# A graph network's edge-list search: bf16 one-hots from doubled keys, and five long gathers in place of fifty

## The chip, the core and the metric

The kernel runs on one core of a Trainium2 chip. The metric is the device time of one execution, in microseconds (us); the time of a kernel is the median over its runs. The engines are TensorE (PE; its weight loads are listed as PEld), VectorE (DVE), ScalarE (ACT), GpSimd (POOL) and the queue engine SyncE (SP), which only issues transfers here.

## The reference, cut to what matters

Four graph layers run one after the other on 3,125 nodes with 128 features; each is a layer norm and a ReLU, a layer, and a residual sum. The graph has 103,125 edges, given as `src` and `dst`, sorted by `dst`:

```python
edge_index = jnp.stack([src, dst])
h = jnp.maximum(_layernorm(x, axis=-1), 0.0)
x = x + _L0_gnn_ref(h, edge_index, L0_gnn_W, L0_gnn_b)          # degree-normalized sum over edges
h = jnp.maximum(_layernorm(x, axis=-1), 0.0)
x = x + _L1_gnn_ref(h, src, dst, L1_gnn_Wq, L1_gnn_Wk, L1_gnn_Wv)  # 4 attention heads over edges
h = jnp.maximum(_layernorm(x, axis=-1), 0.0)
x = x + _L2_gnn_ref(h, edge_index, edge_weight, ...)            # two weighted layers
h = jnp.maximum(_layernorm(x, axis=-1), 0.0)
x = x + _L3_gnn_ref(h, edge_index, edge_attr_16, ...)           # messages from edge attributes
```

All of them need to know which edges end in which node. The change touches only how the kernel finds and fetches these lists at its start.

## The kernel before, in words

The program is a row of blocks. Between two blocks all engines meet at a barrier. Inside a block every engine has its own stream of instructions, ordered by hand with semaphores.

**Block 1, `window_starts` (L157 to L327), finds where each window's edges begin.** A window is five neighbouring destination nodes, and there are 625 windows. The sorted `dst` is loaded as 125 partitions x 825 columns. SP issues that load and the load of `x`, then the copies of `src`, `dst` and `edge_weight` into `scratch_table` in memory (4,125 rows of 3 x 25 values, L315), then one border edge for each partition (L318) and two edges of each edge group (L320, L321), which add to `ends_in`, and last the table's padding (L322). DVE casts `dst` to f32, works out the window of each edge with two `floor_div`s (L113, L114), and splits it into `win_hi` (0 to 24) and `win_lo` (0 to 24, L239). In five pieces of 165 columns it compares both with 0 to 24 (L244), which makes the bf16 one-hots `one_hi` and `one_lo`. Each DVE operation is "linked": the engine waits for its semaphore before the next. For each piece PE multiplies the one-hots, five columns at a time (`GRP`), into `pairs_ps` (L294, 33 matmuls a piece). Then DVE waits for `ends_in`, makes three small tests of the input (`falls`, `wide`, L253 to L257), waits for PE, masks `pairs` (L260), and a short chain of small operations of DVE and PE gives the first table row of each window (L265 to L274), which SP writes to `scratch_starts` (L325).

**Block 2, `edge_slots` (L370 to L505), fetches each window's edges.** SP loads the starts (L419) and then the layers' weights. POOL makes three iotas and waits for `index`. DVE waits for the iotas and the starts and works out `index` = start + 0 to 9 (L445). Then POOL issues 50 gathers (L433), for each of `BLOCKS` = 5 blocks of 125 windows ten (`GROWS`), each of which fetches one table row of 75 values (300 bytes) for each of 125 partitions:

```python
            for b in range(BLOCKS):
                for j in range(GROWS):
                    nc.gpsimd.indirect_dma_start(rows[:, b, j, :], None, table, ...)
```

Meanwhile DVE runs the first layer norm (`layer_norm_relu`, L130 to L139) and keeps the transposed weights (`keep_weights`, L362 to L367); ACT scales the normalized rows (L153). Then, for each block b, DVE waits for its gathers and copies them out to `flat` (L456, three copies), PE transposes `flat` in two halves of three transposes (L486) into two halves of PSUM, and ACT copies each half out (L498, three copies). PE waits before half n until ACT has copied half n - 2. When all are copied, DVE makes the keys and weights (L459 to L474).

**Block 3, `adjacency` (L508 on),** builds the count matrices in bf16. It starts with the first comparison into `hot` (L607), which reads bf16 keys stored twice next to each other and bf16 `steps`. After it come the layers; nothing in them is touched.

## Time and profile before

| | |
|---|---|
| Time, median of 3 runs | 3521.36 us (3520.54 to 3534.1) |
| The profiled execution's own time | 3524.91 us |
| Its span, first to last instruction | 3523.2 us |
| Busy: PE, DVE, ACT, POOL | 2461.0, 1738.8, 1209.0, 1837.8 us |
| First comparison of the `adjacency` block starts at | 166.75 us |

The profiled execution's time is 1.71 us longer than its span and 3.55 us (0.1%) above the median. All places in time are microseconds from the start of the span. Busy shares over the whole span tell little here: the stages of the program follow one another, and each has its own limit.

### The profile page before, as it was taken

To read this page: it belongs to the slowest core of one execution; us is meant where nothing else is said; L and a number is where in the kernel's file an instruction comes from. 1 tells how busy PE (TensorE), PEld (TensorE's weight loads), DVE (VectorE), ACT (ScalarE), POOL (GpSimd) and SP (SyncE) were. 2 spreads that over 40 slices of the span, in tenths; PEclk is the share of its full clock that TensorE was granted. 3 is DMA by queue.
4 is the path that set the end of the run, shared out by engine and by line. 5 is a ranking of instruction groups with operands and counts; after the bars stand their busy time and mean duration, and the time that the engine had idled before them with its cause. 6 is when DMAs were issued, how large, how long until landed. Compare 5 with 4: busy or idle time off the path is not lost. (4 is left out here: it accounts for less than half of the span.)

```text
span 3523.2 us, 60853 instructions
## 1 busy us (share of the span) xinstructions
PE 2461.0 (70%) x19676; PEld 1710.3 (49%) x19676; DVE 1738.8 (49%) x3577; ACT 1209.0 (34%) x2123; POOL 1837.8 (52%) x1601
## 2 busy tenths in 40 slices
PE   2176776768588878878779998266666666666666
PEld 2166666634255555555554454144444444444444
DVE  8399999934487787888871113111111111111112
ACT  1166666611587787787860001000000000000000
POOL 2500000000688888888840000377777777777776
PEclk7599999979699999999999998555555555555555
DMA  4045555573211111111119784312222222222122
GB/s 50 17 146 180 177 177 177 176 202 98 71 49 43 46 46 47 44 49 45 46 43 231 182 203 94 46 48 48 48 48 49 48 48 48 48 49 48 48 48 57
DMA packets 243639, 296.72 MB, mean 84 GB/s; under 512 B 151910, under 2 KB 185517, under 8 KB 240267
## 3 DMA queue, kind: packets, MB, share of 16 engines
q1 hardware_dynamic: 175120, 239.72, 26.6%
q0 software_dynamic: 68400, 55.69, 6.6%
q8 instruction: 41, 0.67, 0.1%
q14 instruction: 78, 0.64, 0.1%
HBM read 191.87 MB, written 103.70 MB: 84 GB/s over the span
## 5 line engine op out<-in xcount | busy, mean ns | idle before, releaser
L2047 POOL DMA_INDIRECT gathered_rows<-scratch_projected,index x825 | 997.6, 1209 | 310.3 <-issue 213.7
L1617 POOL TENSOR_TENSOR score<-score,rise 125x500 f32<-125x500 f32 (+1 forms) x609 | 672.2, 1139 | 44.8 <-DVE peaks L1553 40.8
L2104 PE MATMUL sums<-hot,message 125*128 125x32 f32 x1650 | 386.2, 403 | 360.7 <-DVE message L2131 360.7
L2104 PEld LDWEIGHTS sums<-hot,message 125*128 125x128 f32 x1650 | 364.2, 329 | 514.3 <-DVE message L2131 346.3
L1617 POOL TENSOR_TENSOR H<-H,rise 125x500 f32<-125x500 f32 (+1 forms) x91 | 103.3, 1135 | 818.2 <-DVE peaks L1553 815.6
L2095 PE MATMUL factor<-mix,attrT 80*125 80x320 f32 x660 | 412.0, 778 | 57.7 <-ACT attrT L2065 57.7
L2065 ACT COPY attrT<-attr_flipped 80x125 f32<-80x125 f32 x165 | 43.0, 260 | 1181.2 <-PE attr_flipped L2091 1181.2
L2131 DVE TENSOR_TENSOR message<-gathered_rows,factor 125x640 f32<-125x640 f32 x165 | 135.5, 821 | 592.3 <-DMA gathered_rows<-scratch_projected,index 592.3
L1553 DVE CUSTOM_DVE_ANT_0 score<-raw,log_in 125x500 f32<-125x500 f32 (+1 forms) x609 | 353.9, 619 | 133.4 <-PE raw L1438 80.7
L1453 PE MATMUL probsT<-ident,score 125*125 125x125 f32 x2175 | 349.5, 288 | 30.5 <-ACT score L1509 12.4
L1500 ACT ACTIVATE rise<-raw 125x1000 f32<-125x1000 f32 (+1 forms) x350 | 313.9, 917 | 150.3 <-DVE peaks L1553 77.6
L1453 PEld LDWEIGHTS probsT<-ident,score 125*125 125x125 f32 x2175 | 289.2, 195 | 107.8 <-DVE weighed L1574 66.6
L667 PE MATMUL built<-pair_weight,hot 125*128 125x125 bf16 x3750 | 256.7, 232 | 113.9 <-DVE pair_weight L614 113.9
L667 PEld LDWEIGHTS built<-pair_weight,hot 125*128 125x128 bf16 x3750 | 234.7, 105 | 131.8 <-DVE pair_weight L614 131.8
L614 DVE TENSOR_TENSOR pair_weight<-hot,w_parts 125x3840 bf16<-125x3840 bf16 x125 | 269.7, 2158 | 17.2
L2095 PEld LDWEIGHTS factor<-mix,attrT 80*125 80x125 f32 x660 | 191.0, 320 | 172.1 <-ACT attrT L2065 105.7
L1438 PE MATMUL raw<-QT,key 32*125 32x500 f32 (+1 forms) x1400 | 194.4, 625 | 92.1 <-DVE peaks L1553 89.1
L1574 DVE COPY weighed<-probsT 125x500 f32<-125x500 f32 x400 | 251.0, 672 | 13.9 <-PE probsT L1453 13.9
L1509 ACT ACTIVATE score<-score,shift 125x3125 f32<-125x3125 f32 x87 | 252.5, 2903 | 0.0
L2137 DVE TENSOR_TENSOR acc<-acc,sums 128x32 f32 x165 | 31.1, 188 | 421.4 <-PE sums L2104 421.4
L1964 POOL MEMSET mix<- 80x640 f32 x1 | 0.6, 628 | 392.9 <-POOLq L1168 392.9
L607 DVE TENSOR_TENSOR hot<-keys,steps 125x2560 bf16<-125x2560 bf16 x125 | 185.5, 1484 | 0.3 <-PEq L375 0.3
(225 smaller groups left out, 3266.2 us busy)
## 6 DMA issues: line engine op xcount, KB each, us to landing
weights_in<-scratch_weightsT SPq DMA_DIRECT2D x50, 1093.8 KB
scratch_weightsT<-wT SPq DMA_DIRECT2D x25, 1367.2 KB
scratch_logs<-log SPq DMA_DIRECT2D x75, 437.5 KB
log_in<-scratch_logs SPq DMA_DIRECT2D x150, 218.8 KB
counts_in<-scratch_counts SPq DMA_DIRECT2D x25, 683.6 KB
scratch_counts<-cc SPq DMA_DIRECT2D x24, 683.6 KB
gathered_rows<-scratch_projected,index POOLq DMA_INDIRECT x825, 3.3
attr<-in_edge_attr SPq DMA_DIRECT2D x165, 39.1 KB
```

The lines of the kernel that those rows point to most:

```text
L614: nc.vector.tensor_tensor(pair_weight[:, b].rearrange("p k g (a e) -> p k g a e", e=2), pair.unsqueeze(1).broadcast_to([P, 3, G, FULL // 2 ...
L667: ins = nc.tensor.matmul(built[b][:, 256 * w + P:256 * w + 2 * P], hot[:, q, 0, 2 * w + h], pair_weight[:, b, k, 2 * w + h, 0:P], start=(h ...
L1438: ins = nc.tensor.matmul(raw[:, h, 0:w], key[head, u, :], QT[head, at:at + w], start=True, stop=True)
L1453: ins = nc.tensor.transpose(probsT[:, b, h * P:(h + 1) * P], score[u][h][:, a * P:(a + 1) * P], ident[0:P, 0:P])
L1500: nc.scalar.activation(rise[:, b, heads, 0:width[g]], raw[:, heads, 0:width[g]], ACT.Relu, scale=1.0 / SLOPE - 1.0).then_inc(risen, 1)
L1509: nc.scalar.activation(score[u][h], score[u][h], ACT.Exp, bias=shift[:, u, h:h + 1], accum_out=total[:, u, h:h + 1]).then_inc(exped, 1)
L1553: nc.vector.tensor_tensor_reduce(out=score[u][h][:, at:at + w], in0=raw[:, h, 0:w], in1=log_in[:, at:at + w], scale=1.0, scalar=-3e38, op0 ...
L1574: nc.vector.tensor_copy(weighed[:, a % RING].rearrange("p h d -> p (h d)"), probsT[:, a % 3, 0:PW]).then_inc(moved_dve, 1)
L1617: nc.gpsimd.tensor_tensor(score[u][h][:, at:at + w], score[u][h][:, at:at + w], rise[:, b, h, 0:w], ALU.add).then_inc(added, 1)
L2047: nc.gpsimd.indirect_dma_start(gathered[:, u, k, :], None, projected, bass.IndirectOffsetOnAxis(ap=index[:, u, k:k + 1], axis=0)).then_inc ...
L2095: ins = nc.tensor.matmul(factor[u][:, h, 0:EG * D // 2], attrT[:, u, :], mix[:].rearrange("r c d -> r (c d)")[:, h * EG * D // 2:(h + 1) * ...
L2104: ins = nc.tensor.matmul(sums[:], message[:, u, k, :], hot[:, u, k, :], start=(k == 0), stop=(k == EG - 1))
```

## The change

In block 1 the keys `win_hi` and `win_lo` are written as bf16, each value twice next to itself (`key_hi`, `key_lo`). The comparisons read these and a bf16 iota, in pairs of elements; they make rows of 26 columns instead of 25. The columns are padded from 825 to 828 with keys of -1, and cut into nine pieces of 92. The comparisons are no longer linked to one another: each adds to `ones_made`. PE takes four columns a matmul (104 x 104) instead of five (125 x 125), so 23 matmuls a piece and 207 in all instead of 165. In block 2 each window's ten table rows, which lie next to one another in memory, are fetched as one run of 750 values (3,000 bytes) from a view of the table as single elements, so there are five gathers. `index` is the start times 75, and the iota, the two casts and the sum that made the ten indices are gone.

```diff
+    JOINT, PIECES = 4, 9
+    WIDE = TILES + 1
+    PADDED = (CHUNKS + JOINT - 1) // JOINT * JOINT
+    SIDE = JOINT * WIDE
...
-        one_hi = e(nc.sbuf_tensor(unique("one_hi"), [P, CHUNKS, TILES], BF16))
-        one_lo = e(nc.sbuf_tensor(unique("one_lo"), [P, CHUNKS, WPT], BF16))
+        key_hi = e(nc.sbuf_tensor(unique("key_hi"), [P, PADDED, 2], BF16))
+        key_lo = e(nc.sbuf_tensor(unique("key_lo"), [P, PADDED, 2], BF16))
+        one_hi = e(nc.sbuf_tensor(unique("one_hi"), [P, PADDED, WIDE], BF16))
+        one_lo = e(nc.sbuf_tensor(unique("one_lo"), [P, PADDED, WIDE], BF16))
+        iota_short = e(nc.sbuf_tensor(unique("iota_short"), [P, WIDE], BF16))
...
             dve.wait_ge(pool_done, 11)
+            nc.vector.tensor_copy(iota_short[:], iota_i[:, 0:WIDE])
+            nc.vector.memset(key_hi[:, CHUNKS:, :], -1.0)
+            nc.vector.memset(key_lo[:, CHUNKS:, :], -1.0)
...
             floor_div(nc, link, win_hi[:], win_lo[:], WPT)
-            link(nc.vector.scalar_tensor_tensor(win_lo[:], win_hi[:], -float(WPT), win_lo[:], ALU.mult, ALU.add))
-            step = CHUNKS // 5
-            for k in range(5):
+            both = lambda x: x[:].unsqueeze(2).broadcast_to([P, CHUNKS, 2])
+            link(nc.vector.tensor_copy(key_hi[:, 0:CHUNKS, :], both(win_hi)))
+            link(nc.vector.scalar_tensor_tensor(key_lo[:, 0:CHUNKS, :], both(win_hi), -float(WPT), both(win_lo), ALU.mult,
+                                                ALU.add))
+            step = PADDED // PIECES
+            each = iota_short[:].rearrange("p (a e) -> p a e", e=2).unsqueeze(1).broadcast_to([P, step, WIDE // 2, 2])
+            for k in range(PIECES):
                 part = slice(k * step, (k + 1) * step)
-                for one, win in ((one_hi, win_hi), (one_lo, win_lo)):
-                    link(nc.vector.tensor_tensor(one[:, part, :],
-                                                 win[:, part].unsqueeze(2).broadcast_to([P, step, TILES]),
-                                                 iota[:, 0:TILES].unsqueeze(1).broadcast_to([P, step, TILES]),
-                                                 ALU.is_equal))
-                marks["one", k] = count[0]
+                for one, key in ((one_hi, key_hi), (one_lo, key_lo)):
+                    nc.vector.tensor_tensor(one[:, part, :].rearrange("p c (a e) -> p c a e", e=2),
+                                            key[:, part].unsqueeze(2).broadcast_to([P, step, WIDE // 2, 2]), each,
+                                            ALU.is_equal).then_inc(ones_made, 1)
...
-            per = CHUNKS // GRP
+            per = PADDED // JOINT
             for k in range(per):
-                if k % (per // 5) == 0:
-                    pe.wait_ge(dve_done, marks["one", k // (per // 5)])
+                if k % (per // PIECES) == 0:
+                    pe.wait_ge(ones_made, 2 * (k // (per // PIECES) + 1))
...
-            nc.gpsimd.iota(off_i[:], [[1, GROWS]], base=0, channel_multiplier=0).then_inc(pool_ready, 1)
...
+            runs = table.rearrange("r (e o) -> (r e) o", o=1)
             pool.wait_ge(index_ready, 1)
             for b in range(BLOCKS):
-                for j in range(GROWS):
-                    nc.gpsimd.indirect_dma_start(rows[:, b, j, :], None, table,
-                                                 bass.IndirectOffsetOnAxis(ap=index[:, j, b:b + 1], axis=0)
-                                                 ).then_inc(gathered[b], 16)
+                nc.gpsimd.indirect_dma_start(rows[:, b].rearrange("p j r -> p (j r)"), None, runs,
+                                             bass.IndirectOffsetOnAxis(ap=index[:, b:b + 1], axis=0)
+                                             ).then_inc(gathered[b], 16)
...
-            dve.wait_ge(pool_ready, 3)
+            dve.wait_ge(pool_ready, 2)
             nc.vector.tensor_copy(steps[:], steps_i[:])
-            link(nc.vector.tensor_copy(off_f[:], off_i[:]))
             dve.wait_ge(loaded, 16)
-            link(nc.vector.tensor_copy(row_f[:], row0[:]))
-            nc.vector.tensor_tensor(index[:], row_f[:].unsqueeze(1).broadcast_to([P, GROWS, BLOCKS]),
-                                    off_f[:].unsqueeze(2).broadcast_to([P, GROWS, BLOCKS]),
-                                    ALU.add).then_inc(index_ready, 1)
+            nc.vector.tensor_scalar(index[:], row0[:], float(KINDS * ROW), None, ALU.mult).then_inc(index_ready, 1)
...
             for b in range(BLOCKS):
-                dve.wait_ge(gathered[b], 16 * GROWS)
+                dve.wait_ge(gathered[b], 16)
```

The masks `fold` and `same`, `pairs` and the two PSUM tiles behind it change from 125 to 104 columns, and `hist` (L265) sums four blocks of 26 columns instead of five of 25.

## Rows read from the trace of the kernel before

**Rows 1.** Stretches: us, busy and count of PE, PEld, DVE, ACT, POOL; clock, DMA share, GB/s.

```profile
8.90:53.80 44.90, 15.11 (x132) 14.37 (x132) 44.58 (x10) 0.00 (x0) 0.00 (x0) 0.78 0.63 37
84.80:148.40 63.60, 8.11 (x30) 6.67 (x30) 3.51 (x16) 6.05 (x31) 47.15 (x39) 0.50 0.13 24
166.75:3523.20 3356.45, 2431.41 (x19465) 1683.99 (x19465) 1647.53 (x3420) 1189.31 (x2063) 1771.51 (x1533) 0.76 0.34 87
```

**Rows 2.** Timeline of block 1: start us, us, engine, line, operation, tiles, count.

```profile
4.72 0.59 DVE L236 CAST win_lo<-dst_i 125x825 f32<-125x825 int32 x1
...
7.85 1.02 DVE L239 SCALAR_TENSOR_TENSOR win_lo<-win_hi,win_lo 125x825 f32<-125x825 f32 x1
...
8.90 4.46 DVE L244 TENSOR_TENSOR one_hi<-win_hi,iota 125x4125 bf16<-125x4125 f32 x1
...
24.96 7.99 SPq L318 DMA_DIRECT2D dst_i<-in_dst  x1
...
34.53 0.81 SPq L321 DMA_DIRECT2D ends_i<-in_dst  x1
35.38 0.51 SPq L322 DMA_DIRECT2D scratch_table<-pad  x1
...
49.33 4.46 DVE L244 TENSOR_TENSOR one_lo<-win_lo,iota 125x4125 bf16<-125x4125 f32 x1
53.83 1.02 DVE L253 TENSOR_TENSOR falls<-dst_i 125x825 f32<-125x825 int32 x1
...
53.84 3.79 PE L294 MATMUL pairs_ps<-one_lo,one_hi 125*125 125x125 bf16 x33 [5.21 <-DVE one_lo L244]
...
56.32 0.15 DVE L257 TENSOR_REDUCE faults<-wide 33x1 f32<-33x5 f32 x1
57.74 0.29 DVE L260 TENSOR_TENSOR pairs<-pairs_ps,same 125x125 f32<-125x125 f32 x1 [1.27 <-PE pairs_ps L294]
```

**Rows 3.** Two more stretches of block 1, columns as in rows 1.

```profile
37.20:37.40 0.20, 0.20 (x5) 0.20 (x4) 0.20 (x1) 0.00 (x0) 0.00 (x0) 0.50 0.71 6
37.40:37.60 0.20, 0.20 (x5) 0.20 (x4) 0.20 (x1) 0.00 (x0) 0.00 (x0) 0.50 0.02 0
```

**Rows 4.** The comparisons of block 3: ns min/median/max, first and last start us.

```profile
L607 DVE TENSOR_TENSOR hot<-keys,steps x125: 1480/1484/1493, 166.8 to 707.5; 125x2560 bf16<-125x2560 bf16 x125
```

**Rows 5.** Timeline of block 2, columns as in rows 2.

```profile
67.33 0.21 DVE L445 TENSOR_TENSOR index<-row_f,off_f 125x50 int32<-125x50 f32 x1
67.46 2.41 DVE L130 BATCH_NORM_STATS2 stats<-X 125x6 f32<-125x128 f32 x12
...
67.87 1.41 POOL L433 DMA_INDIRECT rows<-scratch_table,index  x1 [1.12 <-DVE index L445]
...
80.42 3.90 ACT L153 ACTIVATE H<-H,rstd 125x128 f32<-125x128 f32 x13 [2.78 <-DVE rstd L139]
...
81.87 0.41 DVE L367 TENSOR_TENSOR bias<-parts 1x256 f32<-1x256 f32 x1
...
84.83 0.49 DVE L456 CAST flat<-rows 125x250 f32<-125x250 int32 x2 [2.55 <-DMA rows<-scratch_table,index]
...
85.57 1.62 PE L486 MATMUL turned<-ident,flat 125*125 125x125 f32 x6 [16.36 <-DVE flat L456]
...
87.55 0.29 ACT L498 COPY weight<-turned 125x125 f32<-125x125 f32 x1
```

**Rows 6.** The gathers: ns min/median/max, first and last start us; time to landing.

```profile
L433 POOL DMA_INDIRECT rows<-scratch_table,index x50: 1205/1209/1405, 67.9 to 142.3; - x50
...
DMA to landing us min/median/max: 2.8/3.0/3.2
```

**Rows 7.** DMA engines in 40 slices of 85.5 to 87.1 us: busy share, tenths.

```profile
DMA  0062000000000000000000000000292289000002
```

**Rows 8.** Timeline where the last block of windows has been copied.

```profile
148.38 0.81 DVE L459 CAST outside<-win_i 125x1250 f32<-125x1250 int32 x1 [2.35 <-ACT weight L498]
```

More of the change, by code:

```diff
@@ L157, in window_starts @@
 def window_starts(nc, T, table, starts, X, ident, ones, iota, iota_tile, irregular):
+    JOINT, PIECES = 4, 9
+    WIDE = TILES + 1
+    PADDED = (CHUNKS + JOINT - 1) // JOINT * JOINT
+    SIDE = JOINT * WIDE
+    assert PADDED % (JOINT * PIECES) == 0 and WPT == TILES
     used = []
@@ L177, in window_starts @@
         iota_ti = e(nc.sbuf_tensor(unique("iota_ti"), [P, TILES], I32))
-        fold = e(nc.sbuf_tensor(unique("fold"), [P, TILES], F32))
-        same = e(nc.sbuf_tensor(unique("same"), [P, GRP], F32))
+        fold = e(nc.sbuf_tensor(unique("fold"), [SIDE, WIDE], F32))
+        same = e(nc.sbuf_tensor(unique("same"), [SIDE, JOINT], F32))
         before = e(nc.sbuf_tensor(unique("before"), [TILES, TILES], F32))
-        pairs = e(nc.sbuf_tensor(unique("pairs"), [P, P], F32))
+        pairs = e(nc.sbuf_tensor(unique("pairs"), [SIDE, SIDE], F32))
         hist = e(nc.sbuf_tensor(unique("hist"), [TILES, WPT], F32))
@@ L196, in window_starts @@
         pe_done = sem("pe_done")
+        ones_made = sem("ones_made")
         starts_done = sem("starts_done")
@@ L288, in _ @@
         def _(pe):
-            per = CHUNKS // GRP
+            per = PADDED // JOINT
             for k in range(per):
-                if k % (per // 5) == 0:
-                    pe.wait_ge(dve_done, marks["one", k // (per // 5)])
-                ins = nc.tensor.matmul(pairs_ps[:], one_hi[:, GRP * k:GRP * (k + 1), :].rearrange("p j h -> p (j h)"),
-                                       one_lo[:, GRP * k:GRP * (k + 1), :].rearrange("p j h -> p (j h)"),
-                                       start=(k == 0), stop=(k == per - 1))
+                if k % (per // PIECES) == 0:
+                    pe.wait_ge(ones_made, 2 * (k // (per // PIECES) + 1))
+                here = slice(JOINT * k, JOINT * (k + 1))
+                ins = nc.tensor.matmul(pairs_ps[:], one_hi[:, here, :].rearrange("p j h -> p (j h)"),
+                                       one_lo[:, here, :].rearrange("p j h -> p (j h)"), start=(k == 0),
+                                       stop=(k == per - 1))
             ins.then_inc(pe_done, 1)
@@ L378, in edge_slots @@
         row0 = e(nc.sbuf_tensor(unique("row0"), [P, BLOCKS], I32))
[L379 to L382 removed]
+        index = e(nc.sbuf_tensor(unique("index"), [P, BLOCKS], I32))
         rows = e(nc.sbuf_tensor(unique("rows"), [P, BLOCKS, GROWS, KINDS * ROW], I32))
```

18 lines of the change are left out of this document (7 added, 11 removed).

## The prediction

> **What bounds the kernel now.** I read the timeline first, since the blocks are separated by barriers and busy shares over 3,500 us say nothing of a start that is 5% long. Everything from the first comparison of block 3 at 166.75 us to the end is untouched [rows 1], so the question is how much earlier that instruction starts. I then took each block's start apart by stretches, and asked in each which engine the others wait for.
>
> Block 1 is DVE's: in the 44.90 us from 8.90 to 53.80 us DVE is busy 44.58 with ten comparisons, PE 15.11 [rows 1]. One comparison takes 4.46 us, the ten run end to end, and only then come the three tests (53.83 to 56.47 us); PE's last piece starts at 53.84, takes 3.79 us, and `pairs` (L260) starts at 57.74 after waiting 1.27 us for it [rows 2]. Block 2 is POOL's: from 84.80 to 148.40 us POOL is busy 47.15 of 63.60 us, no other engine over 8.2 [rows 1], and the 50 gathers start from 67.9 to 142.3 us, so one each (142.3 - 67.9)/49 = 1.52 us, of which 1.21 is the instruction [rows 6]. The reader should see in the timeline that layer norm and weights end on DVE at 81.87 + 0.41 = 82.28 us, 2.55 us before the first block of windows is there [rows 5]; after that everybody waits for gathers up to 148.38 us [rows 8].
>
> **Block 1: the comparisons.** Prices first. On f32 keys DVE takes 1.02 us for 825 elements and 4.46 for 4,125 [rows 2]: (4.46 - 1.02)/3,300 = 1.042 ns an element and 0.16 us fixed. The comparison of block 3, which has just the form that the change brings (bf16 in doubled pairs), takes 1.484 us for 2,560 elements [rows 4], less 0.16 that is 0.517 ns each. A new comparison has 92 x 26 = 2,392 elements: 1.40 us. If the pairs bought nothing it would be 2.65. I take 1.40, since form, types and the innermost pair are those of rows 4. Without links the next instruction starts 0.08 us before the last ends: `index` starts at 67.33, takes 0.21, and the next starts at 67.46 [rows 5]. So 18 comparisons take 17 x 1.32 + 1.40 = 23.8 us, against 44.9.
>
> What comes before them: three small unlinked instructions (iota copy, two memsets), at 0.1 us each by the smallest row, 0.15 [rows 2], less the overlap: +0.3, at most 0.45. The keys' cast has 1,650 elements; the cast of 825 takes 0.59 [rows 2], (0.59 - 0.16)/825 = 0.52 ns, so 1.02 us and at most 1.88 at the slow price. I take 1.02, the same kind of operation. `key_lo` is a two-source f32 operation like L239, 1,650 elements: 1.88 in place of 1.02. From 4.72: +0.3, then 3.13 unchanged up to 8.15, 1.06 and 1.92 with their links: the first comparison starts at 11.1 (8.90 before), the last ends at 34.9, at the latest 35.9.
>
> PE: 33 matmuls take 3.79 us, 0.115 each [rows 2]; 23 take 2.6 at that price, 2.2 if they shrink with the columns (104 of 125). DVE makes a piece in 2 x 1.32 = 2.64, so PE keeps up at either price, though at 2.6 only just, and ends by 34.9 + 2.6 = 37.5.
>
> **The wait that comes next.** After its last comparison DVE waits for `ends_in`. Before, this had long come. Now it hasn't: SP issues the last of these transfers only at 34.53 to 35.34 us, because its queue stands behind the table copies (L318 alone holds it 7.99 us) [rows 2], and the DMA engines are still 0.71 busy at 37.3 us and quiet from 37.4 [rows 3]. None of this depends on DVE. Behind this wait on DVE lie the tests and with them `pairs`, and PE waits for that. The landing lies between 35.4 and 37.6; I take 37.3, since these few small packets are queued behind the table's on the same engines. Then the tests, 2.64 us, and `pairs` at 40.0 us, against 57.74: **-17.7 us**. This also covers every uncertainty of DVE's list up to 2.4 us. If the landing were early PE's 37.5 and DVE's 34.9 + 2.64 would be last: `pairs` at 37.6, -20.1. The chain behind `pairs` stays; 104 columns for 125 save less than 0.1.
>
> **Block 2: up to the first gather.** One small iota (POOL) and two small casts (DVE, linked) go, 0.15 + 0.04 us each by the smallest row [rows 2]: some -0.5 us, at most 0.6, nothing if the load of the starts is the last to come. So in the old clock the first gather starts at 67.3, layer norm at 66.9 and DVE is free at 81.7.
>
> **The gathers.** Neither their number of rows per instruction (125) nor POOL's work for one changes if each partition's run is one piece, so 1.52 us apart the five start at 67.3 to 73.4. Each moves 375,000 bytes. Bounds for the transfer: now 42 gathers in 63.60 us at a DMA share of 0.13 [rows 1] cost 0.13 x 16 x 63.6/42 = 3.15 engine-us each for 37,500 bytes; ten times that is 31.5, or 2.0 us on 16 engines. After 166.75 us the engines move 87 GB/s at a share of 0.34, 16 GB/s each [rows 1], so 23.4 engine-us, 1.5 us. With 3.0 us from start to landing as now [rows 6], the last is there at 73.4 + 3.0 + 1.5 = 77.9, or at 67.3 + 3.0 + 5 x 2.0 = 80.3. I take the middle, 79; either is before DVE is free at 81.7. So layer norm, which was hidden behind gathers, becomes the cover, and the transfers cost nothing. If they were twice as slow, the last would come at 90 and still just in time for the fifth block.
>
> Do all 16 engines share a gather? In one slice of 0.04 us the busy share reaches 9 tenths [rows 7], 14 engines at once. The Trainium skill, "DMA: Bandwidth & Descriptors", in "Why a DMA increments its semaphore by 16 and not by 1", says that a DMA uses the largest number up to 16 that divides its outer dimension, here 5 of 125. The trace does not agree for the gathers as they are; by the rule a long gather would take 31.5/5 = 6.3 us at the dearer price.
>
> **From the gathers to the keys.** DVE copies block after block without waiting: three copies in 0.69 us (84.83 on) [rows 5], the first is done at 82.4. PE needs 1.62 for two halves, and ACT ends 87.84 - 85.57 = 2.27 us after PE's start: 1.62 and 0.65 behind it [rows 5]. ACT is free of layer norm only at 84.32 - 0.6 = 83.7, so half 0 is copied at 84.35. Half n waits for the copy of half n - 2, which costs 0.81 (PE) + some 0.25 + 0.6 (ACT) = 1.7 for two halves: four more rounds, 84.35 + 6.8 = 91.15, and half 9 at 92.0. L459, before at 148.38 [rows 8], starts at 92.1: **-56.3 us**. Bounds: PE alone as limit gives 91.2; every block one after the other, 83.7 + 5 x 2.3 = 95.2.
>
> **Sum.** -17.7 - 56.3 = -74.0 us. The first comparison of block 3 starts at 92.7 instead of 166.75. The profiled execution ran 3524.91, so a like one 3450.9; the median is 3.55 lower: **3447.3 us**, -2.1%. Differences under 0.5% (17.6 us) could hardly be told from no change here; this one can.
>
> **The rivals.**
>
> *The wait for `ends_in` costs nothing* (landing before 35 us): 20.1 for 17.7, 3445 us. For it: the transfers are tiny. Against it: issue ends at 35.34, and the engines are full till 37.4 [rows 2, 3]. Chance 0.08.
>
> *Late gathers.* Each pays ten times today's engine time and only five engines carry all: 5 x 31.5/5 = 31.5 us, last landing at 67.3 + 3 + 31.5 = 102, then one block's 3 us: L459 at 105, 3460 us. Against it rows 7. Every engine count between gives less. Chance 0.12 for 3452 to 3475.
>
> *The doubled keys don't do what they should*: comparisons of 2.65 us, 17 x 2.57 + 2.65 = 46.3, end at 57.4, tests, `pairs` at 60.1: block 1 loses 2.4 us, and the total is -53.9: 3467 us. For it: the inner run is 26 columns where that of rows 4 is 128. Chance 0.06.
>
> *The other side: a long gather is cut into single elements.* The new view of the table has a last dimension of 1. If each value becomes a transfer of its own, there are 468,750. In block 1 the 100-byte rows of the table, under 12,400, took 0.63 x 16 x 44.9 = 453 engine-us [rows 1], 37 ns each; 468,750 x 37 ns/16 = 1,080 us, so some 4,450 us in all, more if POOL pays 1.21/125 us for each. It decides against the change as soon as the five gathers take over 96 us (last landing at 163 instead of 145 in the old clock, which eats block 1's gain). Against it: the destination is one run of 3,000 bytes a partition, and in rows 6 75 values travel at one price per row. The Trainium skill, "DMA: Bandwidth & Descriptors", in the same section, says that one descriptor moves one contiguous run of the last dimension; read on the source alone, that speaks for this rival, and no row here tests it. Chance 0.04.
>
> **How the numbers follow.** The forecast as told has 0.70, its own range 3444 to 3452 (PE's lower bound and noise below, 95.2 for 92.1 above). With the early landing (0.08) and the nearer two thirds of the late gathers (0.08), 3440 to 3462 holds about 0.86 on paper; what I leave out are the slow comparisons, the elements and the far end of the late gathers. All but the elements are faster by over 0.5%: 0.95; slower 0.04; within 0.5% 0.01, for long gathers at 60 to 90 us in all.
>
> **What would show it.** Right: 18 comparisons of 1.40 us, the last ending near 35 us; DVE idle for `ends_in` for some 2 us; `pairs` at 40; five gathers of 1.2 us on POOL, no wait of DVE for them after 81.7 in the old clock; L459 some 8 us after the end of ACT's second scaling; block 3 from 92.7 us on as before. Wrong: comparisons of 2.6 us, PE as the releaser of `pairs`, a wait of `flat` on gathers, or a gather on POOL well over 1.5 us. The prediction also fails if later stages don't move along rigidly, for instance at another granted clock; nothing in the rows ties them to a place in time.

## The result, and the profile after

The time fell from 3526.73 us (3520.54 to 3534.1, four runs in all) to 3473.39 us (3469.66 to 3475.32), a ratio of 0.9858 [0.984, 0.9875]: 53 us less, where 74 had been forecast. The direction was right; the size was not, and 3473 lies above the range given. The brackets behind a ratio are its 95% interval.

Block 1 after: the timeline of the changed kernel, with start, duration, and in brackets the idle time and its releaser.

```profile
7.87 1.87 DVE L252 CAST key_hi<-win_hi 125x1650 bf16<-125x1650 f32 x1
9.78 1.88 DVE L253 SCALAR_TENSOR_TENSOR key_lo<-win_hi,win_lo 125x1650 bf16<-125x1650 f32 x1
11.69 1.41 DVE L260 TENSOR_TENSOR one_hi<-key_hi,iota_short 125x2392 bf16<-125x2392 bf16 x1
...
26.20 10.52 SPq L333 DMA_DIRECT2D dst_i<-in_dst  x1
...
34.04 1.40 DVE L260 TENSOR_TENSOR one_lo<-key_lo,iota_short 125x2392 bf16<-125x2392 bf16 x1
...
35.49 1.31 PE L309 MATMUL pairs_ps<-one_lo,one_hi 125*104 125x104 bf16 x23 [0.88 <-DVE one_lo L260]
36.77 1.22 SPq L335 DMA_DIRECT2D ends_i<-in_dst  x1
38.03 0.81 SPq L336 DMA_DIRECT2D ends_i<-in_dst  x1
38.88 0.51 SPq L337 DMA_DIRECT2D scratch_table<-pad  x1
43.27 1.02 DVE L267 TENSOR_TENSOR falls<-dst_i 125x825 f32<-125x825 int32 x1 [7.83 <-DMA ends_i<-in_dst]
...
45.94 0.27 DVE L274 TENSOR_TENSOR pairs<-pairs_ps,same 104x104 f32<-104x104 f32 x1
```

The comparisons take 1.40 us and the last ends at 35.44. PE takes 1.31 us for its last piece, and `pairs` doesn't wait for it. DVE then stands 7.83 us for `ends_in`. The issue of the border edges starts 1.2 us later than before and holds SP for 10.52 us where it took 7.99 [rows 2], so the last of these transfers is issued at 38.84 us instead of 35.34. `pairs` starts at 45.94 instead of 57.74: 11.8 us earlier, 17.7 forecast.

Block 2, same view.

```profile
55.19 0.16 DVE L453 TENSOR_SCALAR index<-row 125x5 int32<-125x5 int32 x1
...
55.68 1.41 POOL L443 DMA_INDIRECT rows<-scratch_table,index  x1 [0.67 <-DVE index L453]
...
61.98 1.21 POOL L443 DMA_INDIRECT rows<-scratch_table,index  x1 [0.30 <-issue]
...
69.37 0.41 DVE L382 TENSOR_TENSOR bias<-parts 1x256 f32<-1x256 f32 x1
69.71 0.47 DVE L462 CAST flat<-rows 125x250 f32<-125x250 int32 x2
...
79.95 0.81 DVE L465 CAST outside<-win_i 125x1250 f32<-125x1250 int32 x1 [7.18 <-ACT weight L504]
...
98.33 1.49 DVE L613 TENSOR_TENSOR hot<-keys,steps 125x2560 bf16<-125x2560 bf16 x1 [0.30 <-PEq L390]
```

The five gathers go as forecast, and the first copy into `flat` follows layer norm with no wait. The keys start 79.95 - 45.94 = 34.0 us after `pairs`, before 148.38 - 57.74 = 90.6 [rows 2, 8]: -56.6 us, forecast -56.3. The gathers' own rows:

```profile
L443 POOL DMA_INDIRECT rows<-scratch_table,index x5: 1209/1213/1407, 55.7 to 62.0; - x5
...
DMA to landing us min/median/max: 7.2/7.5/7.8
```

So the last landed near 61.98 + 7.5 = 69.5 us (an estimate from the median), about when DVE was free. What the transfers used, from the DMA queues between 55 and 71 us (packets, MB, share of 16 engines):

```profile
q0 software_dynamic: 1120, 1.88, 38.4%
```

0.384 x 16 x 16 / 5 = 19.7 engine-us a gather.

Block 3 starts at 98.33 instead of 166.75 us, 68.4 earlier, yet the span fell only by 49.6. The missing 19 us are lost later. From the start of block 3 to the first gather of the edge layer at the end (L2053) it was 2090.1 us and is now 2109.8, and most of that lies in the attention layer, from whose first to last score product it was 890.1 and is 904.8 us. The change doesn't touch this layer. Stretches of 800 us inside it show every engine executing fewer instructions after the change; first before, then after (columns as in rows 1).

```profile
952.00:1752.00 800.00, 645.69 (x7845) 449.20 (x7845) 641.33 (x1770) 633.17 (x709) 685.43 (x623) 0.96 0.17 46
```

```profile
884.00:1684.00 800.00, 646.29 (x7746) 451.10 (x7746) 627.18 (x1742) 621.61 (x700) 673.58 (x613) 0.94 0.17 45
```

No engine is full in either: the busiest, POOL, has 685.43 of 800 us before. TensorE's granted clock, the third value from the end, is lower as well, 0.94 for 0.96. DVE's waits in the same stretches (us in total, times, longest), before and after:

```profile
DVE score L1553 <- issue: 25.2, 14, 2.8
```

```profile
DVE score L1559 <- issue: 30.6, 30, 2.9
```

"Issue" means that nothing which the profile shows holds the engine. Below stand one such row of after (with the one ahead of it), and what the instruction queue q14 moved (packets, MB, share) in those stretches, first before and then after. No view names the engine that q14 serves. I take the packets that differ between kernels for DVE's, since edits of DVE's stream alone change their number (e16 and e17 below).

```profile
1347.04 0.68 DVE L1580 COPY weighed<-probsT 125x500 f32<-125x500 f32 x1
1350.37 0.68 DVE L1559 CUSTOM_DVE_ANT_0 score<-raw,log_in 125x500 f32<-125x500 f32 x1 [2.65 <-issue]
```

```profile
q14 instruction: 56, 0.46, 0.2%
```

```profile
q14 instruction: 55, 0.45, 0.2%
```

This made three theories; the lower clock could be a cause of its own or follow from any of them. **Position**: later stages run slower when they start at another time. **TensorE's stream**: block 1 has 42 more matmuls, so its code lies elsewhere. **VectorE's stream**: the change lengthens DVE's program ahead of block 3 by 8 instructions (45 to 56 in block 1, 121 to 118 in block 2, counted in the program, its waits included), and the attention loop, 330 DVE instructions for two tiles, lies 8 places further on.

### The profile page after: what moved, and what is told of

Same layout as the page of the kernel before. It is cut to its first block and busy times, and to the rows that moved or that the text cites. A ratio compares the mean times of both kernels' runs of the same rounds, so it can differ in the third digit from the quotient of the medians.

```text
span 3473.6 us, 60900 instructions
## 1 busy us (share of the span) xinstructions
PE 2475.7 (71%) x19718; PEld 1722.4 (50%) x19718; DVE 1719.1 (49%) x3587; ACT 1208.9 (35%) x2123; POOL 1782.4 (51%) x1555
## 5 line engine op out<-in xcount | busy, mean ns | idle before, releaser
L2053 POOL DMA_INDIRECT gathered_rows<-scratch_projected,index x825 | 997.0, 1208 | 310.3 <-issue 213.9
L1444 PE MATMUL raw<-QT,key 32*125 32x500 f32 (+1 forms) x1400 | 196.8, 632 | 93.9 <-DVE peaks L1559 90.6
L1580 DVE COPY weighed<-probsT 125x500 f32<-125x500 f32 x400 | 251.0, 672 | 13.4 <-PE probsT L1459 13.1
L2143 DVE TENSOR_TENSOR acc<-acc,sums 128x32 f32 x165 | 31.2, 189 | 421.6 <-PE sums L2110 421.6
```

Source lines behind the costliest of these rows:

```text
L1444: ins = nc.tensor.matmul(raw[:, h, 0:w], key[head, u, :], QT[head, at:at + w], start=True, stop=True)
L1580: nc.vector.tensor_copy(weighed[:, a % RING].rearrange("p h d -> p (h d)"), probsT[:, a % 3, 0:PW]).then_inc(moved_dve, 1)
L2053: nc.gpsimd.indirect_dma_start(gathered[:, u, k, :], None, projected, bass.IndirectOffsetOnAxis(ap=index[:, u, k:k + 1], axis=0)).then_inc ...
```

## The experiments

Each kernel was timed beside the kernel before. "DVE" is the number of DVE instructions added ahead of block 3. "Start saved" is 167.0 us (the mean of 166.75 and 167.2 in two profiles of before) less the start of block 3; "time saved" is the median of before in the same batch less the kernel's (3526.73 for after; 3524.61 for e1 to e4, 3523.95 for e5 to e8, 3528.52 for e9 to e12, 3525.58 for e13 to e16, 3525.32 for e17 and e18); "given back" is the difference of the two. "Attention" is first to last score product in the profile. The start is that of one profiled execution and the times are medians, so a difference of a few us between two entries of "given back" says nothing; the profiled executions of e7 and e1 were 15 and 18 us slower than their medians.

| kernel | DVE | median us | ratio | block 3 starts | start saved | time saved | given back | attention |
|---|---|---|---|---|---|---|---|---|
| after | +8 | 3473.39 | 0.9858 [0.984, 0.9875] | 98.3 | 68.7 | 53.3 | 15.4 | 904.8 |
| e1_keys_alone | +11 | 3512.97 | 0.9967 [0.9953, 0.9981] | 153.6 | 13.4 | 11.6 | 1.8 | 908.8 |
| e2_gathers_alone | -3 | 3469.73 | 0.9845 [0.9828, 0.9862] | 110.1 | 56.9 | 54.9 | 2.0 | 886.5 |
| e3_after_again | +8 | 3465.94 | 0.9829 [0.9813, 0.9844] | 95.1 | 71.9 | 58.7 | 13.2 | 896.4 |
| e4_before_again | 0 | 3523.16 | 0.9999 [0.9987, 1.001] | 167.2 | -0.2 | 1.4 | -1.6 | 892.8 |
| e5_wait16 | +8 | 3483.66 | 0.9893 [0.9867, 0.9919] | 112.6 | 54.4 | 40.3 | 14.1 | 896.6 |
| e6_wait70 | +8 | 3540.26 | 1.0045 [1.0031, 1.006] | 169.0 | -2.0 | -16.3 | 14.3 | 899.1 |
| e7_ends_first | +8 | 3461.74 | 0.9822 [0.9805, 0.9838] | 90.8 | 76.2 | 62.2 | 14.0 | 901.7 |
| e8_not_doubled | +8 | 3484.91 | 0.9881 [0.9859, 0.9903] | 112.8 | 54.2 | 39.0 | 15.2 | 903.9 |
| e9_pe42 | -3 | 3473.76 | 0.9843 [0.9817, 0.9869] | 109.9 | 57.1 | 54.8 | 2.3 | 885.7 |
| e10_dve11 | +8 | 3482.79 | 0.986 [0.9834, 0.9886] | 110.2 | 56.8 | 45.7 | 11.1 | 896.1 |
| e11_pe86 | +8 | 3466.13 | 0.981 [0.9784, 0.9836] | 90.2 | 76.8 | 62.4 | 14.4 | 902.0 |
| e12_pe22 | +8 | 3463.7 | 0.9804 [0.9778, 0.9829] | 90.4 | 76.6 | 64.8 | 11.8 | 903.5 |
| e13_dve120 | +128 | 3456.61 | 0.9796 [0.9772, 0.982] | 90.2 | 76.8 | 69.0 | 7.8 | 887.8 |
| e14_three_pieces | -4 | 3453.79 | 0.9783 [0.9757, 0.9809] | 92.1 | 74.9 | 71.8 | 3.1 | 887.9 |
| e15_pool3 | +5 | 3448.99 | 0.9773 [0.9748, 0.9798] | 90.9 | 76.1 | 76.6 | -0.5 | 885.4 |
| e16_dve60 | +68 | 3416.74 | 0.9688 [0.9664, 0.9713] | 90.4 | 76.6 | 108.8 | -32.2 | 855.7 |
| e17_before68 | +68 | 3493.97 | 0.9914 [0.9894, 0.9934] | 166.8 | 0.2 | 31.4 | -31.2 | 853.0 |
| e18_after60 | +68 | 3431.03 | 0.9733 [0.9712, 0.9754] | 95.7 | 71.3 | 94.3 | -23.0 | 863.3 |

**The parts, and both kernels once more.** e1 is the changed `window_starts` with the old `edge_slots`, e2 the reverse; no line is edited otherwise.

> Only block 1 of the change (bf16 doubled keys, nine pieces, 104 columns); the fifty gathers as before. Shift of the first comparison of block 3, rigid: pairs at 46 as in the changed kernel instead of 57.7, so 11.8 us earlier. Interference theory (the faster comparisons slow the DMA engines beside them): the last border edges arrive at about 43 us again. Scatter theory (DMA time differs between executions): anywhere from 38 to 43. Clock theory by position: attention stage longer than 890 us; by scatter: 885 to 910, no relation. Time: 8 to 14 us below the kernel before.

> Only block 2 of the change (five long gathers); block 1 as before. Block 3 starts 56.7 us earlier. Interference theory: DMA engines quiet at 37.4 us as in the kernel before; scatter theory: 37 to 43. If nothing is given back later the time is 57 us below the kernel before; if the loss of the changed kernel after block 3 (19 us in its profile) comes from standing earlier in time, 40 to 45 us below.

> The changed kernel unaltered, for the scatter of its parts. Interference theory: border edges at 43 us again, block 3 from 98.3 us. Position theory of the clock: attention from the first to the last score product again 905 us and 314 us at the lower clock level between blocks 3 and the edge layer; scatter theory: both move by 10 us or more from execution to execution. Rigid shift alone would make it 68 us faster than the kernel before; its four runs so far say 50 to 54.

> The kernel before, unaltered, for the scatter of its parts. Position theory: attention again 890 us, 270 us at the lower level. Scatter theory: attention 885 to 910 us, the profile so far having been one of the short ones, since two of four runs were 12 us longer than the other two. Time equal to the kernel before within its scatter of 14 us.

The gathers alone move the end as far as the start of block 3, less 2.0 us; both parts together give back 13.2. The loss is no accident of one profile: the repeat of before keeps its time, the repeat of after gives back again. The keys alone don't fit so well: by the medians they give back 1.8 us only, yet in the profile the attention took 908.8. That profile is of the slowest of ten executions (3531.4; the others from 3506.01), so I rest nothing on its times. What it shows of DVE's waits stands in the last part of this section.

**Position, the wait for `ends_in`, and the doubled pairs.** e5 and e6 keep the changed code and hold POOL back in block 2, with 5 and 22 extra iotas:

```diff
+            wait = chained(pool, held)
+            for _ in range(5):
+                wait(nc.gpsimd.iota(win_i[:].rearrange("p (w h) -> p w h", h=2), [[WIN, WINDOWS], [0, 2]], base=0,
+                               channel_multiplier=0))
```

e7 issues `ends_in` before the table copies:

```diff
             start_rows(sp, X[:], T["x"].rearrange("(t p) f -> p t f", p=P), x_in)
-            for k, name in enumerate(("src", "dst", "edge_weight")):
-                column = table[0:ROWS, k * ROW:(k + 1) * ROW]
-                if name == "edge_weight":
-                    column = column.bitcast(F32)
-                sp.dma_start(column, T[name].rearrange("(r e) -> r e", e=ROW)).then_inc(table_done, 16)
             sp.wait_ge(pool_done, 11)
             with nc.allow_non_contiguous_dma(reason="an edge a row, and two of every edge group"):
...
                 sp.dma_start(ends_i[:, 1, :], grouped[:, :, EG * P - 1]).then_inc(ends_in, 16)
+            for k, name in enumerate(("src", "dst", "edge_weight")):
+                column = table[0:ROWS, k * ROW:(k + 1) * ROW]
+                if name == "edge_weight":
+                    column = column.bitcast(F32)
+                sp.dma_start(column, T[name].rearrange("(r e) -> r e", e=ROW)).then_inc(table_done, 16)
```

e8 compares with a key that isn't read in pairs:

```diff
-                    nc.vector.tensor_tensor(one[:, part, :].rearrange("p c (a e) -> p c a e", e=2),
-                                            key[:, part].unsqueeze(2).broadcast_to([P, step, WIDE // 2, 2]), each,
+                    nc.vector.tensor_tensor(one[:, part, :],
+                                            key[:, part, 0:1].broadcast_to([P, step, WIDE]),
+                                            iota_short[:].unsqueeze(1).broadcast_to([P, step, WIDE]),
```

> The changed kernel with five more linked iotas on GpSimd (3.3 us each) ahead of the index: block 3 starts some 16.5 us later, where it starts with the gathers alone (110 us). Position theory (what is lost after block 3 depends on where block 3 stands in time): no loss at this place, so 55 us below the kernel before, 5 us slower than the changed kernel. Added-work theory (the loss comes with the comparisons' change, whatever the place): 60 - 16 = 44 us below. Scatter alone: 44 to 50 below.

> The changed kernel with 22 more linked iotas: block 3 starts some 73 us later, at 168 us, where it starts in the kernel before (167). Position theory: the time of the kernel before within 2 us. Theory that the loss comes with the comparisons' change: 10 to 14 us slower than the kernel before. Scatter alone: equal within 3.

> The changed kernel with the three transfers for ends_in issued ahead of the table copies. The wait of VectorE for them (7.8 us in the profile) goes: tests start with the last comparison at 35.4 to 35.6, pairs at 38.2, so 2 to 7.7 us earlier, unless the table copies, now later, hold SP back before it writes the starts at 41. Time: 3 to 7 us below the changed kernel, 63 to 67 below the kernel before. If the wait had been covered anyway: no difference.

> The changed kernel, but the comparisons read each bf16 key once, repeated by a step of 0 over 26 columns, instead of doubled pairs. If the doubled pair is what makes the fast form: 2,392 x 1.042 ns + 0.16 = 2.65 us a comparison, the last ends at 11.7 + 46.3 = 58.0, pairs at 60.7, 15 us later than in the changed kernel and 3 us later than in the kernel before; time 12 to 18 us above the changed kernel. If bf16 alone is enough: 1.40 us a comparison and no difference.

Position falls. e6 starts block 3 two microseconds after the kernel before does, and still loses 16.3 us; wherever the code of after starts block 3, it gives back 13 to 15. Timeline of e7 and of e8, DVE:

```profile
34.29 1.40 DVE L260 TENSOR_TENSOR one_lo<-key_lo,iota_short 125x2392 bf16<-125x2392 bf16 x1
35.61 1.01 DVE L267 TENSOR_TENSOR falls<-dst_i 125x825 f32<-125x825 int32 x1
...
38.27 0.27 DVE L274 TENSOR_TENSOR pairs<-pairs_ps,same 104x104 f32<-104x104 f32 x1
```

```profile
55.23 2.64 DVE L260 TENSOR_TENSOR one_lo<-key_lo,iota_short 125x2392 bf16<-125x2392 bf16 x1
57.79 1.01 DVE L268 TENSOR_TENSOR falls<-dst_i 125x825 f32<-125x825 int32 x1
...
60.46 0.27 DVE L275 TENSOR_TENSOR pairs<-pairs_ps,same 104x104 f32<-104x104 f32 x1
```

With `ends_in` issued early the wait is gone and `pairs` starts at 38.27, 7.7 us before that of after. In time e7 beats e3 by 4.2 us, which the intervals don't separate. Without pairs a comparison takes 2.64 us and `pairs` starts at 60.46: the rival's 2.65 and 60.1. Then nobody waits for `ends_in`.

**Which stream.** e9 adds 42 small transposes on PE to e2, e11 and e12 86 and 22 of them to e7; e10 adds 11 memsets on DVE to e2.

```diff
+            for _ in range(42):
+                nc.tensor.transpose(spare[0:32, 0:32], ident[0:32, 0:32], ident[0:32, 0:32])
...
+            for k in range(11):
+                nc.vector.memset(spare[:, k:k + 1], 0.0)
             dve.wait_ge(pool_ready, 2)
```

> The kernel with the gathers alone (from the start of block 3 to the edge layer 2092 us), and 42 small transposes more on TensorE in block 2, where it is idle and nobody waits for it; their output is not read. It gives TensorE as many more instructions ahead of block 3 as the change gives it in block 1. Theory of the place in TensorE's instruction stream: the stretch from block 3 to the edge layer becomes 2102 to 2118 us and the time 10 to 16 us longer than with the gathers alone. Theory that VectorE's stream, the memory or the comparisons themselves do it: 2092 again and no difference.

> The kernel with the gathers alone and eleven small memsets more on VectorE at the start of block 2, where it waits 4.6 us for GpSimd; their output is not read. VectorE then has as many instructions ahead of block 3 as in the changed kernel. Theory of VectorE's instruction stream: from block 3 to the edge layer 2102 to 2118 us and 10 to 16 us longer than with the gathers alone. Theory of TensorE's stream: 2092, no difference.

> The changed kernel with the transfers for ends_in first, and 86 small transposes on TensorE in block 2 (output not read), so that with the 42 of block 1 TensorE has 128 matrix instructions more than the kernel before, each with its weight load. Theory of TensorE's stream, if it repeats with 256 instructions: from block 3 to the edge layer 2090 to 2093 us again and the time 12 to 16 us below the version without them, 3446 to 3450. Otherwise 2102 to 2118 and no gain, or 1 us lost if the transposes get in the way.

> The same with 22 small transposes: 64 matrix instructions more than the kernel before. Theory of TensorE's stream, if it repeats with 128 instructions: 2090 to 2093 us from block 3 to the edge layer, as with 86. If it repeats with 256 alone: 2102 to 2118. Other theories: no difference from the version without them.

TensorE's stream falls: 42 more PE instructions change nothing (2.3 given back, as in e2's 2.0), and 86 or 22 on top of +8 cure nothing (14.4 and 11.8). Eleven empty DVE instructions, executed long before, bring the loss into the kernel that hadn't it: 9.0 us more than e9, with the attention 10.4 us longer. The intervals of e9 and e10 overlap; what carries the reading is that all nine kernels with +8 give back 11 to 15 us, and the five with -4 to +5 from -1.6 to 3.1. By its times e1, at +11, doesn't join the first group (1.8).

**Other counts.** All on top of e7. e13 adds two lots of 60 memsets and e16 one. e14 cuts the comparisons into three pieces (`JOINT, PIECES = 4, 3`), twelve instructions fewer. e15 gives the three small preparations to GpSimd:

```diff
+            link(nc.gpsimd.tensor_copy(iota_short[:], iota_i[:, 0:WIDE]))
+            link(nc.gpsimd.memset(key_hi[:, CHUNKS:, :], -1.0))
+            link(nc.gpsimd.memset(key_lo[:, CHUNKS:, :], -1.0))
...
-            dve.wait_ge(pool_done, 11)
-            nc.vector.tensor_copy(iota_short[:], iota_i[:, 0:WIDE])
-            nc.vector.memset(key_hi[:, CHUNKS:, :], -1.0)
-            nc.vector.memset(key_lo[:, CHUNKS:, :], -1.0)
+            dve.wait_ge(pool_done, 14)
```

> The version with the transfers for ends_in first, and 120 small memsets on VectorE in block 2, 60 where it waits for GpSimd and 60 where it waits for ScalarE (output not read): 128 instructions more than in the kernel before. Theory that the place in VectorE's stream counts and repeats with 128: from block 3 to the edge layer 2090 to 2093 us instead of 2102 to 2118. Theory that any added instruction on VectorE costs it: 2102 to 2118. Time: 10 to 16 us below the version without them less what the memsets themselves cost (0 to 3 us), 3449 to 3455; else no gain.

> The version with the transfers first, and the comparisons in three pieces of 276 columns instead of nine of 92: twelve comparisons fewer, so VectorE has 4 instructions fewer than in the kernel before. Theory of the place in VectorE's stream: from block 3 to the edge layer 2090 to 2093 us. Price: TensorE's last piece has 69 matmuls (4 to 6.7 us) and ends after the tests, pairs 1 to 4 us later. Time 8 to 14 us below the version with nine pieces, 3450 to 3456. If the loss belongs to doubled keys or the earlier start: 1 to 4 us slower.

> The version with the transfers first, and its three small preparations (bf16 iota, two memsets) on GpSimd instead of VectorE: 5 instructions more on VectorE than in the kernel before. Theory of the stream: 2090 to 2093 or 2102 to 2118 from block 3 to the edge layer, according to where the border between -3, 0 (no loss) and +8, +11 (loss) lies; nothing between the two levels. In block 1 up to 0.5 us either way.

> The version with the transfers first, and 60 small memsets on VectorE where it waits for GpSimd (output not read): 68 instructions more than in the kernel before. Theory that it repeats with 64 instructions: about as with +4, unknown side; with 128: half a period off, most likely a loss, 2102 to 2118. Any-added-work theory: 2102 to 2118 or more.

e14 and e15 get back nearly all of the rigid gain (3.1 and -0.5 given back). e15 is e7 with three instructions moved from DVE to GpSimd, and the intervals of the two don't overlap: it is the clearest pair for the loss at +8. e13, at +128, has the attention of count 0 (887.8), but its time gives back 7.8, and from the start of block 3 to the edge layer it takes 2100.6 us where its expectation asked for 2090 to 2093: the attention repeats with 128, for the whole time that isn't shown. And e16, with 60 instructions that do nothing, is 45 us faster than e7: 3416.74 us, the fastest kernel here. Its expectation had called a loss most likely. Its attention stretch, DVE's wait for issue, and q14:

```profile
880.00:1680.00 800.00, 654.31 (x8234) 455.05 (x8226) 668.76 (x1851) 659.79 (x743) 716.25 (x651) 0.99 0.17 46
```

```profile
DVE score L1562 <- issue: 0.5, 1, 0.5
```

```profile
q14 instruction: 7, 0.06, 0.0%
```

In the same 800 us DVE executes 1,851 instructions for 1,742, it hardly ever waits for issue, and q14 moves 7 packets instead of 55. The memsets themselves cost nothing, since DVE waits for POOL right behind them (timeline of e16):

```profile
43.56 1.67 DVE L452 MEMSET spare<- 125x1 f32 x58 [0.38 <-issue]
47.13 0.23 DVE L454 CAST steps<-steps_i 125x128 bf16<-125x128 int32 x1 [1.89 <-POOL steps_i L440]
```

**The place alone, and the change at equal place.** The same memsets in the kernel before (68) and in after (60), with nothing else edited: both loops then lie where e16's lies.

> The kernel before, with 68 small memsets on VectorE at the start of block 2, where it waits 4.7 us for GpSimd (output not read). Place theory: from block 3 to the edge layer 2054 us instead of 2091, queue q14 with some 28 fetches in all instead of 78, time 35 to 37 us below the kernel before, 3486 to 3492. If the gain needed the new block 1: no difference.

> The changed kernel with 60 small memsets in the same place, so 68 VectorE instructions more than the kernel before. Place theory: from block 3 to the edge layer 2054 us, time 3526 - 36 - 70 = 3420, and 68 to 72 us below the kernel before with its 68 memsets. If part of the loss has another cause in the change: less than 66 us between the two.

The kernel before gains 31.4 us from 68 memsets alone (attention 853.0). Over the whole span q14 moves 0.24 MB in it, where it moved 0.64: first e17, then before.

```profile
q14 instruction: 29, 0.24, 0.0%
```

```profile
q14 instruction: 78, 0.64, 0.1%
```

At equal place the change itself is worth 3493.97 - 3431.03 = 62.9 us, with block 3 starting 166.8 - 95.7 = 71.1 us earlier. That is less than the expectation asked for: the place explains a part of the gap between 71 and the measured 53, and some 8 us are left. They lie in the attention, which is 863.3 us in e18 and 853.0 in e17. By ACT's copies into `mixed_copy`, one a tile, five tiles of e18 took 35.3 to 38.1 us where the others took 34.2. The next row is a stretch around a long tile of after, the one behind it a stretch of its neighbour (columns as in rows 1; in the clock 0.5 is 1.2 GHz and 1.0 2.4 GHz):

```profile
1252.00:1292.00 40.00, 33.51 (x342) 23.67 (x330) 25.50 (x76) 25.86 (x31) 28.36 (x27) 0.74 0.13 35
1292.00:1332.00 40.00, 32.32 (x409) 22.23 (x409) 33.39 (x93) 34.08 (x37) 36.19 (x33) 1.00 0.17 47
```

PE was partly at the lower level there. What sets off such a dip, no run here isolates. The attention as a whole in before, after, e17 and e18:

```profile
906.60:1796.70 890.10, 700.30 (x8387) 479.93 (x8387) 703.31 (x1950) 693.83 (x777) 765.25 (x694) 0.94 0.17 46
838.60:1743.40 904.80, 713.57 (x8383) 490.03 (x8387) 702.59 (x1950) 694.15 (x777) 764.83 (x694) 0.92 0.17 46
908.20:1761.30 853.10, 680.03 (x8383) 465.56 (x8387) 697.62 (x1950) 691.70 (x777) 765.46 (x694) 0.96 0.18 48
836.00:1699.40 863.40, 686.41 (x8383) 470.36 (x8387) 702.57 (x1950) 691.58 (x777) 764.78 (x694) 0.95 0.17 47
```

The counts are the same up to a few missing records. DVE, ACT and POOL are busy as long in all four; PE's busy time moves with the length.

**DVE's stalls, pass by pass.** DVE's waits for issue alone don't tell kernels with the loss from those without it: e15 has more of them than after, and loses nothing. In e6, which loses, a part is put down to PE's `probsT`. Over the whole attention, e15 first, then after, then e6:

```profile
DVE score L1559 <- issue: 31.1, 28, 2.8
DVE score L1559 <- issue: 30.8, 31, 2.9
DVE score L1559 <- PE probsT L1459: 10.3, 11, 1.0
DVE score L1564 <- issue: 16.5, 23, 2.8
DVE score L1564 <- PE probsT L1464: 23.5, 16, 2.9
```

The single rows explain it. One pass of the attention loop, two tiles, takes some 72 us. First the rows of such waits in a pass of before, then, beside the wait at 1350.37 shown above, those in a pass of after:

```profile
1338.74 0.68 DVE L1553 CUSTOM_DVE_ANT_0 score<-raw,log_in 125x500 f32<-125x500 f32 x1 [2.63 <-issue]
1366.36 0.68 DVE L1553 CUSTOM_DVE_ANT_0 score<-raw,log_in 125x500 f32<-125x500 f32 x1 [0.17 <-issue]
```

```profile
1344.51 0.29 DVE L1559 CUSTOM_DVE_ANT_0 score<-raw,log_in 125x125 f32<-125x125 f32 x1 [0.18 <-issue]
1361.22 0.68 DVE L1559 CUSTOM_DVE_ANT_0 score<-raw,log_in 125x500 f32<-125x500 f32 x1 [1.01 <-PE probsT L1459]
1377.05 0.68 DVE L1559 CUSTOM_DVE_ANT_0 score<-raw,log_in 125x500 f32<-125x500 f32 x1 [0.17 <-issue]
```

Before has ten stalls of 2.6 to 2.8 us, one a pass. After has ten of 2.7 to 2.9 and, at another place of the pass, ten more of 1.0. The other eight kernels with +8 have nine or ten of the second kind as well, e4 and e9 none. e13 at +128 has before's pattern again, e17 has neither, and e1 at +11 has eleven of 1.6 us for after's 1.0. The table groups all profiles: the attention, DVE's waits before `score` put down to issue or `probsT`, and the time at TensorE's lower clock level, summed from the granted clock in windows of 1 us.

| kernels | DVE | attention us | waits before `score` us | lower level us |
|---|---|---|---|---|
| e16, e17, e18 | +68 | 853.0 to 863.3 | 0.0 to 0.5 | 65 to 82 |
| before, e2, e4, e9, e13, e14, e15 | -4 to +5, +128 | 885.4 to 892.8 | 28.0 to 31.1, e14 36.3 | 102 to 130 |
| the nine with +8 | +8 | 896.1 to 904.8 | 40.0 to 41.5 | 119 to 147 |
| e1 | +11 | 908.8 | 45.1 | 164 |

So at +8 DVE stands some 12 us longer and the attention is some 12 us longer. The lower level goes the same way, and whether it only follows from PE's pauses or adds to the loss, no run separates. That the attention can lengthen without these stalls is seen in e18: it stalls as little as e17, has 82 us at the lower level for 65, and is 10.3 us longer.

## Why the prediction came out as it did

**Comparisons, PE's pieces, the gathers' issue, layer norm as cover, the keys' start: right.** 1.40 us from [rows 4], 18 of them, last end at 35.44 for 34.9; from `pairs` to the keys -56.6 for -56.3. The rival's price for undoubled keys held as well (e8). That the gathers would be cut into single elements (the other side) is refuted: a gather used 19.7 engine-us, less even than the bounds of 23.4 to 31.5.

**The landing of a gather: undersized, and covered.** 3.0 + 1.5 to 2.0 us was reckoned, 7.5 measured (7.2 in e2). The last came near 69.5 us, about when DVE wanted the first block (69.71); the fifth was needed only some 2.4 us later. The forecast's "either is before DVE is free" held by less than it looked. The Trainium skill, "DMA: Bandwidth & Descriptors", in "Why a DMA increments its semaphore by 16 and not by 1", gives 5 engines for 125 partitions: with it an estimate is 3.0 + 19.7/5 = 6.9 us, near the 7.5; over 16 engines it would be 4.2. The prediction laid this rule aside on a slice of 0.04 us with a share of 0.9 [rows 7]. So short a slice doesn't count engines: in after the share reads 1.39 from 59.5 to 60.0 us. In e6, where the gathers have the DMA engines to themselves, the end of the last ones reads 0.34 over 1.1 us, which is 5.4 of 16 engines (columns as in rows 1):

```profile
138.10:139.20 1.10, 0.00 (x0) 0.00 (x0) 1.10 (x8) 0.62 (x3) 0.00 (x0) 0.50 0.34 123
```

That speaks for five engines a gather; a single gather wasn't run.

**The cast into `key_hi`: the wrong one of two prices.** 1.87 us for 1.02; the upper bound was 1.88. It cost 0.85 us that the wait behind it hid.

**The wait for `ends_in`: right in kind, too small.** The step that failed is "I take 37.3", on "none of this depends on DVE". The landing was put at 37.3; the tests, which wait for it, began at 43.3, 40.0, 41.6, 41.0, 41.1 and 40.7 us in after, e3, e1, e5, e6 and e18. SP had issued the last of these transfers at 38.84 in after, at 36.88 in e3 and at 37.22 in e4, the old kernel again, where the trace of before had 35.34 [rows 2]. So the issue varies by 2 us from one execution to another, also without the change, and the tests began 3.1 (e3) to 4.4 us (after) behind it, where 2 were reckoned. The term of -17.7 measured -11.8; with e3's 40.0 for 37.3 it would be -15. e7 shows what the wait hangs on, the place of these issues in SP's queue: moved forward, `pairs` starts at 38.3. Whether DVE's denser traffic slows the issue, or whether it merely scatters, isn't settled.

**The sum: "later stages move along rigidly; nothing in the rows ties them to a place in time".** This is the step that cost most. They aren't tied to a place in time (e6), but the attention's speed depends on where its loop lies in DVE's instruction stream. With eight more instructions nine kernels gave back 11 to 15 us, in one of them (e10) by empty instructions alone. Sixty-eight gained 31 us in the old kernel. What the place changes is DVE's stalls, as shown above: none at +68, one of 2.7 us a pass at 0, another of 1.0 us at +8. That a stall is the refill of DVE's instruction memory is supported by q14's packets, which fall from 55 to 7 in 800 us where the stalls are gone, but no view names it. The Trainium skill, "Runtime: NRT & Kernel Launch", in "Instruction fetch mechanics", says that the instruction memory is a FIFO refilled in blocks of 16 KiB, 256 instructions, that crossing a block is mostly hidden, and that a taken branch whose target isn't among the two blocks at hand has to fetch it first and stalls. The traces agree with the stall of a loop that jumps back, once a pass. They don't agree on the size: q14's packets are 0.64 MB / 78 = 8 KB, which by the page's 64 bytes an instruction is 128 of them. With blocks of 256 and two at hand, a loop of 330 would reach into a third block only at 73 neighbouring places of 256, so not both at 0 and at +128; yet e13 has before's stalls and its 78 packets.

A count fits 128, though it is only argued. From e16 to before there are 78 - 28 = 50 packets more, and the loop over pairs of tiles runs eleven times, so it jumps back ten times: five packets each time, and one long stall. A loop of 330 instructions touches three or four stretches of 128, according to where it starts; it would have to be that three stay in the memory and four don't. Why +8 adds a second stall although q14 moves as much (55 packets for 56) is open: that it depends on which instruction of the pass a refill falls on would fit, since its length differs (0.7 us at -4 in e14, 0.3 at +5 in e15, 1.0 at +8, 1.6 at +11), but no run shows it. Nor is a stall's length simply added to the time: e14 keeps an attention of 887.9 us. Open as well are the times of e1 and e13, which don't follow their attention (1.8 and 7.8 us given back).

Smaller: the three runs of before that the forecast started from (3521.36) were on the low side; later batches have 3523.95 to 3528.52, which alone is 3 to 7 us.

## What to carry to other kernels

A long loop can depend on how many instructions the same engine has in front of it. When an edit far away moves a loop that it doesn't touch, compare "issue" waits and the instruction queue's packets in both traces before looking for contention, and try a few dozen empty instructions in a spot where the engine waits anyway: here that was worth 31 us on the kernel before and 45 on e7, against 63 for the change itself at equal place. Don't go by the "issue" label alone: look at single rows of one pass, since the same stall can be put down to an engine that is long done. And when an engine gets faster, find the next semaphore that it waits for, and price the queue in front of that transfer with its scatter, or move it forward, as e7 does.

## What the runs showed of the hardware

- A DVE cast from f32 into doubled bf16 with a source broadcast in its innermost step takes 1.87 us for 1,650 elements, 1.04 ns each and 0.16 fixed; an ordinary cast has half of that [rows 2].
- A comparison of bf16 keys broadcast without pairs has the price of f32 (2.64 us for 2,392 elements); read in pairs, even with a run of only 26 columns, 1.40.
- 3,000 bytes for each of 125 partitions in one indirect transfer cost 19.7 engine-us and 1.21 us of GpSimd, no more of the latter than 300 bytes [rows 6].
- DVE's place in its stream: 56 packets of q14 and 25.2 us of waits for issue in 800 us at one place, 7 packets and 0.5 us at another. A loop of 330 DVE instructions stalls 2.7 us a pass at one place, 2.7 and 1.0 at a place 8 instructions on, and not at all 68 on.
- The share of the DMA engines in a window under a microsecond can read over 1 (1.39 in 0.5 us), so it doesn't count engines.
